# Causal attention between two quantised feed-forward blocks: two PSUM banks for scores, four for maxima, and one maximum operation for two heads

## The chip, the cores and the metric

The kernel runs on one core of a Trainium2 chip. The metric is the device time of one execution in microseconds (us); lower is better. TensorE is called PE here, VectorE DVE, ScalarE ACT, GpSimd POOL, and SP is the engine that issues the DMAs.

## The reference

The input is one sequence of 2048 tokens with 256 channels. A feed-forward block with 4-bit weights, causal attention with 16 heads of 16 channels, and the feed-forward block again are each added to it:

```python
x = x + 0.5 * ffn(layernorm(x))       # gate, up: 256 -> 2048, gelu(gate) * up, down: 2048 -> 256
x = x + attention(layernorm(x))       # 16 heads of 16 channels, causal softmax over 2048 keys
x = x + 0.5 * ffn(layernorm(x))       # weights: codes of 4 bits from a table, a scale for each 32
```

## The kernel before

The kernel is written engine by engine: each has a list of instructions in a fixed order, and semaphores with constant counts tie the lists together. Three stretches matter here.

**The first feed-forward block.** Twelve weight tiles are decoded (jobs 0 to 11). For each, ACT takes the bytes of the codes (`take_byte`) and the scales (`widen`), PE transposes both, ACT takes the codes back (`take_turned`), and DVE unpacks them (`decode`, five operations), scales them (`scale_weight`) and, after ACT has rounded them to a high part (`weight_high`), takes the low part (`weight_low`). The layer norm of the first 512 tokens (`variance`, `root`, `norm`, PE's `turn`, `split`) lies between jobs 0 and 1. The gate and up products (`gate_up`) start when the low parts of jobs 0 and 1 and that of the tokens are there. Each needs 128 of the 512 columns of a job.

**The attention.** It walks through 160 steps d. A step takes one group of four heads, one tile of 512 queries and one block of 128 keys. PE makes the scores of each head (`score(d, j)`, j = 0 to 3, keys by queries), ACT takes their exponential (L1175, `prob`), and PE multiplies the step before with the values (`weigh(d - 1)`, L815). The softmax needs the row maximum of each query ahead of its first step, so PE also makes the scores the other way round (`maxima(n)`, n = 0 to 639: one head, 128 queries, up to 512 keys), and DVE takes the maximum of each from PSUM: by a reduction off the diagonal (L1365), by an operation with the mask on it (L1368). Four or five `maxima` are placed in each step (`quota`), behind the scores j of the step by `CUTS`. For the steps with five the places are one, one, two, one; with four, one behind each score. The last one is step 136. PE's order in a step is so: score 0, maximum, score 1, maximum, score 2, one or two maxima, score 3, maximum, `weigh`.

PSUM has eight banks of 512 columns. In the attention, banks 3 to 5 hold scores (`S0`, `SBANKS`), banks 0 to 2 maxima (`M0`, `MBANKS`), bank 6 the output (`O0`), bank 7 the transposes (`X0`). Score n is written when exponential n - 3 is done, maximum n when the DVE has read maximum n - 3:

```python
elif SBANKS <= n < 4 * TAIL:
    pe.wait_ge(s["exp"], n - SBANKS + 1)
...
if n >= N_EARLY + N_BRIDGE + MBANKS:
    pe.wait_ge(s["max_read"], n - MBANKS + 1)
```

**The bridge.** In steps 3 to 7 banks 0 and 1 still hold the projection of the last 512 tokens (`LAST_UNITS`: four units at (4, 1), (5, 0), (6, 0) and (6, 2), where (d, j) is a step and the place behind its score j). The twelve maxima of these steps (`BRIDGE`) all go through bank 2. `last_block` is DVE's order there. When the fourth unit is done, SP writes the projections out and loads queries and keys, with many DMAs one behind the other, up to the row of maxima (`max_row(2)`) for which step 12 waits.

Of the kernel before, what the change touches and what calls it, by code (L numbers as in the profile page):

```python
# [45 lines left out]
SBANKS = 3  # L46
MBANKS = 3
# [5 lines left out]
def build_program(nc, h, Wq, bq, Wk, bk, Wv, bv, Wo, bo, gW, gS, uW, uS, dW, dS, out):  # L53
# [6 lines left out]
    with outer:  # L60
# [67 lines left out]
        def program(s, t):  # L128
# [53 lines left out]
            def chunk_order(n):  # L182
# [9 lines left out]
            BRIDGE = {(4, 0): 1, (4, 2): 1, (5, 0): 1, (5, 2): 1, (5, 3): 1, (6, 0): 1, (6, 1): 1, (6, 3): 1,  # L192
                      (7, 0): 1, (7, 1): 1, (7, 2): 1, (7, 3): 1}
# [90 lines left out]
            S0, M0, O0, X0 = 3, 0, 6, 7  # L284
# [21 lines left out]
            with ExitStack() as st:  # L306
# [85 lines left out]
                with nc.Block() as block:  # L392
# [217 lines left out]
                    def _(pe):  # L610
# [40 lines left out]
                        def gate_up(b, q, m):  # L651
                            k = b * NQ + q
                            if k >= 2:
                                pe.wait_ge(s["product"], k - 1)
                            elif m == 1:
                                pe.wait_ge(s["weight"], 2)
                            g, o = q // GT, (q % GT) * P
                            if b == 0 and q % GT == 0:
# [100 lines left out]
                        def maxima(n):  # L759
# [6 lines left out]
                            if n >= N_EARLY + N_BRIDGE + MBANKS:  # L766
                                pe.wait_ge(s["max_read"], n - MBANKS + 1)
                            elif n > N_EARLY:
                                pe.wait_ge(s["max_read"], min(n, N_EARLY + N_BRIDGE))
                                if n >= N_EARLY + N_BRIDGE:  # L770
                                    pe.wait_ge(s["full"], NU * NB)
                                    pe.wait_ge(s["v"], SUB * NB)
# [48 lines left out]
                        def gather(g):  # L821
                            pe.wait_ge(s["o_copied"], g + 1)
                            pe.wait_ge(s["x_free"], gather_use[g])
                            for i in range(SUB):
# [178 lines left out]
                    def _(act):  # L1003
# [31 lines left out]
                        def weight_high(n):  # L1035
                            act.wait_ge(s["weight"], n + 1)
                            nc.scalar.activation(w_hi[:, n, :, :], weight[:, n % 2, :, :], ACT.Copy).then_inc(s["w_hi"], 1)
# [80 lines left out]
                        for n in range(2):  # L1118
                            take_byte(n)
                            widen(n)  # L1120
                            take_turned(n)
                        root(0)
                        weight_high(0)
                        split(0)
                        weight_high(1)
                        take_byte(2)
                        widen(2)
                        for b in range(NB):
# [110 lines left out]
                    def _(dve):  # L1239
# [10 lines left out]
                        def scale_weight(n):  # L1250
                            dve.wait_ge(s["value"], n + 1)
                            dve.wait_ge(s["turned_s"], n + 1)
                            if n >= 2:
                                dve.wait_ge(s["w_lo"], n - 1)
                            nc.vector.scalar_tensor_tensor(weight[:, n % 2], mag[:, n % 2].bitcast(F16), 2.0 ** 14,
                                                           psum[:, decode_banks(n)[1], :].unsqueeze(1).broadcast_to([P, PL, BT]),
                                                           ALU.mult, ALU.mult).then_inc(s["weight"], 1)

                        def weight_low(n):
                            dve.wait_ge(s["w_hi"], n + 1)  # L1260
                            nc.vector.tensor_tensor(w_lo[:, n], weight[:, n % 2], as_f32(w_hi[:, n]), ALU.subtract).then_inc(s["w_lo"], 1)
# [91 lines left out]
                        def maxima(n):  # L1353
# [9 lines left out]
                            dve.wait_ge(s["max_scored"], n + 1)  # L1363
                            if c < qt:
                                nc.vector.tensor_reduce(to, psum[:, bank, :], AX.X, ALU.max).then_inc(s["max_read"], 1)  # L1365
                            else:
# [113 lines left out]
                        def last_block(d, mine):  # L1480
# [3 lines left out]
                            if d == 4:  # L1484
                                first_rest(u)
                                maxima(mine[1])
# [3 lines left out]
                            if d == 5:  # L1490
                                first_rest(u + 1)
                                maxima(mine[1])
# [10 lines left out]
                            if d == 7:  # L1503
                                third_part(u + 3)
                                maxima(mine[1])
# [147 lines left out]
```

## Time and profile before

| | |
|---|---|
| time, median of 3 runs | 1105.14 us (1104.61 to 1107.93) |
| the profiled execution's own time | 1102.31 us |
| its span, first to last instruction | 1100.6 us |
| mean granted clock of PE | 0.995 of full |
| PE busy | 1051.6 us (96%) |
| DVE busy | 692.0 us (63%) |
| ACT busy | 562.9 us (51%) |

The profile is one execution. A busy PE counts the modelled length of a matmul, which overlaps with the next one, so it is no measure of how far PE is from its best pace; the distances between starts are. L12 is line 12 of the kernel before.

### The profile page before, as it was taken

How to read it: one execution, taken by the hardware profiler on the slowest of the kernel's cores; microseconds unless marked ns; L12 is line 12 of the kernel's file. 1: busy time of each engine (PE TensorE's matmuls, PEld its weight loads, DVE VectorE, ACT ScalarE, POOL GpSimd, SP SyncE). 2: the span in 40 equal slices, each digit the busy share in tenths (PEclk: the TensorE clock that was granted, in tenths of full speed). 3: DMA queues.
4: the chain of work that ended last, by engine and by line, in shares of the span. 5: the costliest groups of instructions: out<-in, count | busy, mean ns of one | idle time of the engine just before them, and what ended most of it. 6: DMA issues, size and time to landing. Idle time of an engine off the chain costs nothing.

```text
span 1100.6 us, 16821 instructions
## 1 busy us (share of the span) xinstructions
PE 1051.6 (96%) x6240; PEld 673.0 (61%) x6240; DVE 692.0 (63%) x1589; ACT 562.9 (51%) x1028; POOL 95.6 (9%) x337
## 2 busy tenths in 40 slices
PE   4999999999998789999999999999999999999998
PEld 3888888887776423332223333333448888888887
DVE  5986544446566488899898988985424434343333
ACT  5664443442344646666667777777663334233222
POOL 0000000000002035221101102111110000000000
PEclk9999999999999989999999999999999999999999
DMA  7001040042140651212013012010000000000000
GB/s 198 2 1 34 1 134 1 10 139 55 27 129 14 168 122 35 69 50 54 1 34 73 16 39 54 2 39 2 1 1 1 1 20 1 1 20 1 20 1 20
DMA packets 85155, 43.75 MB, mean 40 GB/s; under 512 B 47954, under 2 KB 85074, under 8 KB 85074
## 3 DMA queue, kind: packets, MB, share of 16 engines
q1 hardware_dynamic: 85074, 42.69, 14.9%
q8 instruction: 49, 0.80, 0.3%
q14 instruction: 32, 0.26, 0.1%
HBM read 25.63 MB, written 16.78 MB: 39 GB/s over the span
## 4 chain that ended last, share of the span: by engine, by line
PE 79%; DVE 11%; ACT 2%; issue 2%; DMA 2%; SPq 2%; POOL 1%; ACTq 0%; POOLq 0%; DVEq 0%
PE psum L882 16%; PE psum L663 15%; PE psum L815 9%; PE psum L756 9%; PE psum L774 8%; PE psum L899 8%; PE psum L678 8%; DVE attn_part_max L1365 8%; PE psum L710 2%; PE psum L858 1%; PE psum L123 1%; DMA qk_rows<-qkv_parts 1%; ACT attn_prob L1180 1%; PE psum L722 1%; DMA attn_q<-attn_max_rows 1%
## 5 line engine op out<-in xcount | busy, mean ns | idle before, releaser
L1175 ACT ACTIVATE attn_prob<-psum 128x512 f32<-128x512 f32 (+3 forms) x548 | 257.0, 537 | 138.4 <-PE psum L756 135.7
L1365 DVE TENSOR_REDUCE attn_part_max<-psum 128x1 f32<-128x512 f32 x384 | 236.1, 683 | 13.7 <-PE psum L774 12.7
L663 PE MATMUL psum<-ffn_xt,all_w_hi 128*128 128x512 f32 x512 | 166.0, 406 | 0.0
L815 PE MATMUL psum<-attn_prob,attn_vals 128*32 128x512 f32 (+3 forms) x1280 | 151.2, 545 | 2.1 <-POOL attn_prob L585 0.8
L1368 DVE CUSTOM_DVE_ANT_0 attn_junk<-psum,attn_mask 128x128 bf16<-128x128 f32 (+3 forms) x256 | 114.6, 488 | 41.9 <-PE psum L774 41.1
L1471 DVE TENSOR_TENSOR ffn_act_out<-ffn_act_out,psum 128x512 f32<-128x512 f32 x64 | 44.1, 689 | 111.9 <-ACT ffn_act_out L1216 111.7
L1216 ACT ACTIVATE ffn_act_out<-psum 128x512 f32<-128x512 f32 x64 | 38.3, 598 | 130.1 <-PE psum L882 130.1
L663 PEld LDWEIGHTS psum<-ffn_xt,all_w_hi 128*128 128x128 f32 x512 | 91.5, 189 | 17.2
L678 PE MATMUL psum<-all_w_hi,ffn_inner 128*128 128x256 f32 x512 | 101.7, 283 | 0.1
L663 PE MATMUL psum<-ffn_xt,all_w_lo 128*128 128x512 f32 x256 | 101.6, 397 | 0.0
L899 PE MATMUL psum<-all_w_hi,ffn_inner 128*128 128x256 f32 x512 | 100.3, 280 | 0.1
L585 POOL TENSOR_SCALAR_AFFINE_SELECT attn_prob<-attn_prob 128x128 f32<-128x128 f32 x256 | 71.3, 292 | 312.6 <-ACT attn_prob L1175 264.6
L1060 ACT ACTIVATE ffn_act_out<-psum 128x512 f32<-128x512 f32 x64 | 38.2, 598 | 101.2 <-PE psum L663 101.0
L1304 DVE TENSOR_TENSOR ffn_inner<-ffn_act_out,ffn_inner 128x512 fp32r<-128x512 f32 x64 | 44.2, 691 | 71.2 <-ACT ffn_inner L1066 71.0
L678 PEld LDWEIGHTS psum<-all_w_hi,ffn_inner 128*128 128x128 f32 x512 | 82.6, 188 | 2.6 <-issue 0.4
L899 PEld LDWEIGHTS psum<-all_w_hi,ffn_inner 128*128 128x128 f32 x512 | 82.4, 188 | 2.9 <-DVE ffn_inner L1466 0.3
L882 PE MATMUL psum<-ffn_xt_even,all_w_hi 128*128 128x512 f32 x256 | 80.6, 396 | 0.0
L882 PE MATMUL psum<-ffn_xt_odd,all_w_hi 128*128 128x512 f32 x256 | 80.5, 395 | 0.0
L1466 DVE TENSOR_TENSOR ffn_inner<-ffn_act_out,ffn_inner 128x512 fp32r<-128x512 f32 x64 | 44.2, 691 | 52.0 <-ACT ffn_inner L1222 52.0
L678 PE MATMUL psum<-all_w_lo,ffn_inner 128*128 128x256 f32 x256 | 71.5, 279 | 0.0
L899 PE MATMUL psum<-all_w_lo,ffn_inner 128*128 128x256 f32 x256 | 71.5, 279 | 0.0
L1222 ACT ACTIVATE ffn_inner<-ffn_act_out 128x512 fp32r<-128x512 f32 x64 | 40.4, 632 | 52.9 <-PE psum L899 52.2
(148 smaller groups left out, 1618.6 us busy)
## 6 DMA issues: line engine op xcount, KB each, us to landing
qk_rows<-qkv_parts SPq DMA_DIRECT2D x16, 384.0 KB, 2.5
qk_rows<-qkv_parts SPq DMA_DIRECT2D x16, 256.0 KB, 3.0
attn_q_early<-qk_rows SPq DMA_DIRECT2D x8, 384.0 KB, 3.5
attn_k_early<-qk_rows SPq DMA_DIRECT2D x8, 384.0 KB, 4.7
attn_vals<-v_rows SPq DMA_DIRECT2D x48, 64.0 KB, 3.8
attn_k<-qk_rows SPq DMA_DIRECT2D x8, 384.0 KB, 3.7
attn_q<-qk_rows SPq DMA_DIRECT2D x8, 384.0 KB, 3.6
attn_k_late<-qk_rows SPq DMA_DIRECT2D x8, 384.0 KB, 3.5
```

Of the source, the lines that this page charges most:

```text
L585: nc.gpsimd.affine_select(out=tile, in_=tile, compare_op=ALU.is_ge, fill=0.0, base=0, pattern=[[1, P]], channel_multiplier=-1).then_inc(s[ ...
L663: last = nc.tensor.matmul(psum[:, 2 * m + q % 2, :], w_part[a][:, 3 * g + m, pl, o:o + P], xt[:, b % 2, c, pl, :], start=(n == 0), stop=(n ...
L678: last = nc.tensor.matmul(psum[:, ACC + i // 2, (i % 2) * H:(i % 2 + 1) * H], inner[:, a, q % 2, i * P:(i + 1) * P], w_part[e][:, 3 * (c / ...
L756: nc.tensor.matmul(psum[:, score_bank(n), at:BT], keys(key_load(g, c))[part, j, o * P:(o + 1) * P], queries(g)[part, j, at:BT], start=True ...
L774: nc.tensor.matmul(psum[:, max_bank(n), 0:cols], queries(g)[0:KR, hd, i * P:(i + 1) * P], keys(r)[0:KR, hd, 0:cols], start=True, stop=True ...
L815: last = nc.tensor.matmul(psum[32 * hd:32 * hd + 32, O0, at:BT], vals[:, r % KSLOTS * SUB + kb % SUB, VALUES_AT[hd]:VALUES_AT[hd] + 32], p ...
L882: last = nc.tensor.matmul(psum[:, 2 * m + q % 2, :], w_part[a][:, 3 * g + m, pl, o:o + P], xt2[b % 2][:, c, pl, :], start=(n == 0), stop=( ...
L899: last = nc.tensor.matmul(psum[:, ACC + i // 2, (i % 2) * H:(i % 2 + 1) * H], inner2[:, a, q % 2, i * P:(i + 1) * P], w_part[e][:, 3 * (c ...
L1175: nc.scalar.activation(prob[:, n % PRING, at:BT], psum[:, score_bank(n), at:BT], ACT.Exp).then_inc(s["exp"], 1)
L1304: nc.vector.tensor_tensor(inner[:, 1, k % 2, :], act_out[:, k % 2, :], as_f32(inner[:, 0, k % 2, :]), ALU.subtract).then_inc(s["inner_lo"], 1)
L1365: nc.vector.tensor_reduce(to, psum[:, bank, :], AX.X, ALU.max).then_inc(s["max_read"], 1)
L1368: nc.vector.tensor_tensor_reduce(out=junk[:, hd % 2, 0:cols], in0=psum[:, bank, 0:cols], in1=mask[:, BT - cols:BT], scale=1.0, scalar=STAR ...
```

## The change

Scores get two banks (4 and 5) instead of three, maxima four (0 to 3) instead of three. Score n now waits for exponential n - 2. Off the diagonal the maxima of heads 0 and 1, or 2 and 3, of a group lie in neighbouring banks, and DVE reduces both by one operation of two times 512 columns, when both are there; PE waits for banks only at the first of two. At the bridge there are eight maxima (in steps 4 to 6) instead of twelve, which alternate between banks 2 and 7; the others move to step 7, where four banks are free. In the start the norm comes ahead of job 0 on DVE, the first 128 columns of jobs 0 and 1 are scaled and split on their own (`first_scale`, `first_high`, `first_low`) and their other 384 afterwards, and a square root of a constant stands at the head of ACT's list.

```diff
-SBANKS = 3
-MBANKS = 3
+SBANKS = 2
+MBANKS = 4
...
-            BRIDGE = {(4, 0): 1, (4, 2): 1, (5, 0): 1, (5, 2): 1, (5, 3): 1, (6, 0): 1, (6, 1): 1, (6, 3): 1,
-                      (7, 0): 1, (7, 1): 1, (7, 2): 1, (7, 3): 1}
+            BRIDGE = {(4, 0): 2, (5, 0): 1, (5, 1): 1, (5, 3): 1, (6, 0): 1, (6, 1): 1, (6, 3): 1}
...
-            S0, M0, O0, X0 = 3, 0, 6, 7
+            S0, M0, O0, X0 = 4, 0, 6, 7
...
-                return 2 if n < N_EARLY + N_BRIDGE else M0 + n % MBANKS
+                return (2, X0)[n % 2] if n < N_EARLY + N_BRIDGE else M0 + n % MBANKS
...
-                            if b == 0 and q % GT == 0:
+                            if k == 0:
+                                pe.wait_ge(s["first_w_lo"], m + 1)
+                            elif b == 0 and (q == 1 or q % GT == 0):
...
                             if n >= N_EARLY + N_BRIDGE + MBANKS:
-                                pe.wait_ge(s["max_read"], n - MBANKS + 1)
+                                if hd % 2 == 0:
+                                    pe.wait_ge(s["max_read"], n - MBANKS + 2)
...
+                            elif n >= N_EARLY + 2:
+                                pe.wait_ge(s["max_read"], n - 1)
...
-                            dve.wait_ge(s["max_scored"], n + 1)
-                            if c < qt:
+                            pair = c < qt and n >= N_EARLY + N_BRIDGE
+                            if not pair or hd % 2:
+                                dve.wait_ge(s["max_scored"], n + 1)
+                            if pair and hd % 2:
+                                nc.vector.tensor_reduce(part_max[:, g % 2, hd - 1:hd + 1, i, c:c + 1], psum[:, bank - 1:bank + 1, :],
+                                                        AX.X, ALU.max).then_inc(s["max_read"], 2)
+                            elif c < qt and not pair:
...
+                        nc.scalar.activation(deviation[:, TT - 1:TT], nc.const_aps.tensor(1.0, [P, 1], F32), ACT.Sqrt)
...
                         variance(0)
+                        norm(0)
                         decode(0)
-                        norm(0)
+                        first_scale(0)
+                        decode(1)
+                        first_scale(1)
+                        split(0)
+                        first_low(0)
+                        first_low(1)
                         scale_weight(0)
-                        decode(1)
+                        scale_weight(1)
                         weight_low(0)
-                        split(0)
-                        scale_weight(1)
                         weight_low(1)
```

On DVE, late in the attention, behind the row maximum of a group (L1375 before, L1416 now), these rows stood before (`attn_part_max` is the tile of the maxima, L1365 the reduction off the diagonal; a row with x38 is 38 such operations in a row):

```order
L1375 TENSOR_REDUCE attn_row_max<-attn_part_max 128x16
L1365 TENSOR_REDUCE attn_part_max<-psum 128x1 x26
L1388 RECIPROCAL attn_rden<-psum 128x16
L1392 TENSOR_TENSOR all_heads<-psum,attn_rden 128x4x2x16 x2
L1365 TENSOR_REDUCE attn_part_max<-psum 128x1 x38
```

And these stand there now:

```order
L1416 TENSOR_REDUCE attn_row_max<-attn_part_max 128x16
L1403 TENSOR_REDUCE attn_part_max<-psum 128x2 x13
L1429 RECIPROCAL attn_rden<-psum 128x16
L1433 TENSOR_TENSOR all_heads<-psum,attn_rden 128x4x2x16 x2
L1403 TENSOR_REDUCE attn_part_max<-psum 128x2 x19
```

Each two reductions became one with two results; nothing else moved in that stretch, and PE's list in it is as before.

On DVE at the bridge (steps 4 and 5; `qkv_rest` and `qkv_parts` belong to the projection, the rows of L1368 are maxima with their mask) these rows stood before:

```order
L1368 ISA attn_junk,attn_part_max<-psum,attn_mask 128x128
L1368 ISA attn_part_max 128x1
L1336 TENSOR_TENSOR qkv_rest<-qkv_full,qkv_parts 128x512
L1368 ISA attn_junk,attn_part_max<-psum,attn_mask 128x128
L1368 ISA attn_part_max 128x1
L1331 TENSOR_TENSOR qkv_rows_v<-psum,qkv_bias_v 128x256 x2
L1340 TENSOR_TENSOR qkv_parts<-qkv_rest,qkv_parts 128x512
```

And now:

```order
L1409 ISA attn_junk,attn_part_max<-psum,attn_mask 128x128
L1409 ISA attn_part_max 128x1
L1409 ISA attn_junk,attn_part_max<-psum,attn_mask 128x128
L1409 ISA attn_part_max 128x1
L1372 TENSOR_TENSOR qkv_rest<-qkv_full,qkv_parts 128x512
L1367 TENSOR_TENSOR qkv_rows_v<-psum,qkv_bias_v 128x256 x2
L1376 TENSOR_TENSOR qkv_parts<-qkv_rest,qkv_parts 128x512
```

The second maximum moved ahead of the work that waits for ACT's part of the projection.

On ACT at the start, up to the first high part of the weights, these rows stood before:

```order
L1008 ACT_TABLE_LOAD
L1008 ACTIVATE decode_byte<-decode_early_codes 128x512
L1021 ACTIVATE attn_q_early<-decode_scales 128x512
L1032 ACTIVATE decode_turned<-psum 128x512
L1008 ACTIVATE decode_byte<-decode_early_codes 128x512
L1021 ACTIVATE attn_q_early<-decode_scales 128x512
L1032 ACTIVATE decode_turned<-psum 128x512
L1043 ACT_TABLE_LOAD
L1043 ACTIVATE all_deviation<-all_var_eps 128x4
L1037 ACTIVATE all_w_hi<-decode_weight 128x1024
L1054 ACTIVATE ffn_xt<-psum 128x1024
```

And now:

```order
L1132 ACT_TABLE_LOAD
L1132 ACTIVATE all_deviation<-const-float32-1.0 128x1
L1016 ACTIVATE decode_byte<-decode_early_codes 128x512
L1029 ACTIVATE attn_q_early<-decode_scales 128x512
L1057 ACTIVATE all_deviation<-all_var_eps 128x4
L1040 ACTIVATE decode_turned<-psum 128x512
L1016 ACTIVATE decode_byte<-decode_early_codes 128x512
L1029 ACTIVATE attn_q_early<-decode_scales 128x512
L1040 ACTIVATE decode_turned<-psum 128x512
L1051 ACTIVATE all_w_hi<-decode_weight 128x2x128
L1068 ACTIVATE ffn_xt<-psum 128x1024
```

The square root of the norm moved ahead of five activations, and the second load of a table is gone.

## Rows read from the trace of the kernel before

**Rows 1.** The page's part 2: granted clock of PE in 40 equal slices
```profile
PEclk9999999999999989999999999999999999999999
```

**Rows 2.** Windows: start:end, length, busy us (x instructions) of each engine, PEclk, DMA share
```profile
448.00:588.00 140.00, 135.74 (x793) 41.65 (x792) 127.66 (x304) 89.83 (x189) 22.47 (x85) 1.00 0.16 38
588.00:760.00 172.00, 170.17 (x1053) 55.16 (x1049) 148.72 (x359) 124.28 (x266) 25.42 (x97) 1.00 0.14 33
```

**Rows 3.** The page's part 4, the chain that ended last, by line
```profile
PE psum L882 16%; PE psum L663 15%; PE psum L815 9%; PE psum L756 9%; PE psum L774 8%; PE psum L899 8%; PE psum L678 8%; DVE attn_part_max L1365 8%; PE psum L710 2%; PE psum L858 1%; PE psum L123 1%; DMA qk_rows<-qkv_parts 1%; ACT attn_prob L1180 1%; PE psum L722 1%; DMA attn_q<-attn_max_rows 1%
```

**Rows 4.** Timeline, step with five maxima: start, length, engine, line [idle before]
```profile
563.50 0.39 PE L756 MATMUL psum<-attn_q_early,attn_k 99*128 99x512 bf16 x1
...
563.73 0.38 PE L774 MATMUL psum<-attn_k_early,attn_q 96*128 96x512 bf16 x1
...
563.99 2.15 ACT L1175 ACTIVATE attn_prob<-psum 128x512 f32<-128x512 f32 x4 [0.78 <-PE psum L756]
...
564.15 3.08 DVE L1365 TENSOR_REDUCE attn_part_max<-psum 128x1 f32<-128x512 f32 x5 [0.36 <-PE psum L774]
...
565.49 0.10 PEld L774 LDWEIGHTS psum<-attn_k_early,attn_q 96*128 96x128 bf16 x1 [0.49 <-DVE attn_part_max L1365]
...
565.81 1.06 PE L815 MATMUL psum<-attn_prob,attn_vals 128*32 128x512 f32 x8
...
566.81 0.39 PE L756 MATMUL psum<-attn_q_early,attn_k 99*128 99x512 bf16 x1
```

**Rows 5.** Timeline, a step with four maxima off the diagonal
```profile
710.49 1.06 PE L815 MATMUL psum<-attn_prob,attn_vals 128*32 128x512 f32 x8
...
711.98 2.06 ACT L1175 ACTIVATE attn_prob<-psum 128x512 f32<-128x512 f32 x4 [0.78 <-PE psum L756]
...
712.62 0.10 PEld L756 LDWEIGHTS psum<-attn_q_early,attn_k_late 99*128 99x128 bf16 x1 [0.15 <-ACT attn_prob L1175]
...
713.34 0.64 PE L815 MATMUL psum<-attn_prob,attn_vals 128*32 128x512 f32 x4
```

**Rows 6.** Timeline, `weigh` before and behind a step with four diagonal maxima
```profile
657.20 1.06 PE L815 MATMUL psum<-attn_prob,attn_vals 128*32 128x512 f32 x8
...
659.83 0.64 PE L815 MATMUL psum<-attn_prob,attn_vals 128*32 128x512 f32 x4
```

**Rows 7.** Lines by form, 440 to 760 us: count, busy us, mean ns
```profile
L1365 DVE TENSOR_REDUCE attn_part_max<-psum 128x1 f32<-128x512 f32 x336 | 206.2, 683 | 10.9 <-PE psum L774 10.0
L1175 ACT ACTIVATE attn_prob<-psum 128x512 f32<-128x512 f32 x328 | 171.7, 605 | 66.1 <-PE psum L756 65.3
```

**Rows 8.** Lines by form, 0 to 20 us
```profile
L1299 DVE TENSOR_TENSOR ffn_xt<-psum,ffn_xt 128x1024 fp32r<-128x1024 f32 x1 | 1.2, 1221 | 0.0
```

**Rows 9.** Timeline of the start
```profile
7.29 0.17 DVE L1276 TENSOR_SCALAR all_var_eps<-all_mean_var 128x4 f32<-128x4 f32 x1
...
8.46 0.29 DVE L1243 TENSOR_SCALAR attn_q_early<-decode_turned 128x512 uint16<-128x512 uint16 x1 [1.00 <-ACT decode_turned L1032]
...
9.39 0.69 DVE L1248 TENSOR_TENSOR attn_q_early<-attn_q_early,attn_vals 128x1024 uint16<-128x1024 uint16 x1
...
10.26 1.28 ACT L1043 ACT_TABLE_LOAD   x1
...
12.00 1.38 DVE L1292 TENSOR_SCALAR ffn_xb<-all_x,all_mean_var,all_rstd 128x256 f32<-128x256 f32 x4
...
21.50 1.20 PE L663 MATMUL psum<-ffn_xt,all_w_hi 128*128 128x512 f32 x2
...
27.75 0.29 DVE L1243 TENSOR_SCALAR attn_q_early<-decode_turned 128x512 uint16<-128x512 uint16 x1
```

**Rows 10.** Timeline of the bridge: a maximum's wait, and the fourth unit
```profile
363.08 0.23 PE L774 MATMUL psum<-attn_k,attn_q 96*128 96x128 bf16 x1 [0.49 <-DVE attn_part_max L1368]
...
371.94 1.75 PE L710 MATMUL psum<-ffn_xt,qkv_wt 128*128 128x512 f32 x6
```

**Rows 11.** The chain that ended last, in order of time: start, length
```profile
393.12 5.85 DMA attn_q<-attn_max_rows
```

More of the change, by code:

```diff
@@ L766, in maxima @@
                             if n >= N_EARLY + N_BRIDGE + MBANKS:
-                                pe.wait_ge(s["max_read"], n - MBANKS + 1)
[L768 to L772, printed above, removed]
+                                if hd % 2 == 0:
+                                    pe.wait_ge(s["max_read"], n - MBANKS + 2)
+                            elif n >= N_EARLY + N_BRIDGE:
+                                pe.wait_ge(s["max_read"], N_EARLY + N_BRIDGE)
+                                pe.wait_ge(s["full"], NU * NB)
+                                pe.wait_ge(s["v"], SUB * NB)
+                            elif n >= N_EARLY + 2:
+                                pe.wait_ge(s["max_read"], n - 1)
+                            elif n == N_EARLY + 1:
+                                pe.wait_ge(s["x_free"], turn_use[EARLY - 1] + 1)
                             cols = BT if c < qt else P * (i + 1)
@@ L1036, in weight_high, with first_high @@
                             act.wait_ge(s["weight"], n + 1)
-                            nc.scalar.activation(w_hi[:, n, :, :], weight[:, n % 2, :, :], ACT.Copy).then_inc(s["w_hi"], 1)
+                            cols = slice(P if n < 2 else 0, GT * P)
+                            nc.scalar.activation(w_hi[:, n, :, cols], weight[:, n % 2, :, cols], ACT.Copy).then_inc(s["w_hi"], 1)
+                        def first_high(n):
+                            act.wait_ge(s["first_weight"], n + 1)
+                            nc.scalar.activation(w_hi[:, n, :, 0:P], weight[:, n, :, 0:P], ACT.Copy).then_inc(s["first_w_hi"], 1)
                         def root(use):
@@ L1116, in copy_max @@
                             act.sem_inc(s["max_rows"], 1)
[L1118 to L1121, printed above, removed]
+                        nc.scalar.activation(deviation[:, TT - 1:TT], nc.const_aps.tensor(1.0, [P, 1], F32), ACT.Sqrt)
+                        take_byte(0)
+                        widen(0)
                         root(0)
-                        weight_high(0)
+                        take_turned(0)
+                        take_byte(1)
+                        widen(1)
+                        take_turned(1)
+                        first_high(0)
                         split(0)
-                        weight_high(1)
+                        first_high(1)
                         take_byte(2)
                         widen(2)
+                        weight_high(0)
+                        weight_high(1)
                         for b in range(NB):
@@ L1484, in last_block @@
                             if d == 4:
+                                maxima(mine[1])
                                 first_rest(u)
-                                maxima(mine[1])
                                 take_rows(i)
@@ L1490, in last_block @@
                             if d == 5:
+                                maxima(mine[1])
                                 first_rest(u + 1)
-                                maxima(mine[1])
                                 take_rows(i + 2)
@@ L1571, in _ @@
                                 split(Q_USE[NB - 1])
+                            if d == 7:
+                                third_part(NU * NB - 1)
                             if (d, 0) in BRIDGE:
@@ L1615, in build_program @@
         NORM = "aggr var std rstd xb "
-        W_SEMS = "ident turned_s wide turned_c byte turned weight w_hi w_lo step value scales0 scales1 scales2 "
+        W_SEMS = "first_weight first_w_hi first_w_lo ident turned_s wide turned_c byte turned weight w_hi w_lo step value scales0 scales1 scales2 "
         CODE_SEMS = " ".join(f"codes{n}" for n in range(3 * NG))
```

32 lines of the change are left out of this document (21 added, 11 removed).

## The prediction, made before the changed kernel had run

> **What bounds the kernel now.** I read the chain that ended last, the windows, the timeline of single steps, and then the waits at the start and the bridge. The chain lies on PE nearly everywhere; the one other line with a large share is DVE's reduction L1365 with 8% [rows 3]. In the attention two stretches differ. In the steps with five maxima DVE is the bound: the five reads take 3.08 us of a step of 3.31 (563.50 to 566.81), and PE waits 0.49 us for a bank of the last maximum [rows 4]. In the steps with four, PE is the bound: 2.85 from one weigh to the next, and the fourth score's bank comes free (712.62) before PE gets to it [rows 5]. ACT has 2.06 us of exponentials in such a step and is nowhere the bound. Steps 28 to 136 fill 448 to 760 us, 312 us of the span, at full clock [rows 2].
>
> So the change relieves DVE in the five-maxima steps, and takes a bank from the scores in all of them. Which of the two counts is settled by following a step.
>
> **A step's recurrence.** Times from score 0. From the rows: matmuls of 512 columns follow each other by 0.22; an exponential begins 0.49 after its score (563.50, 563.99), DVE's read 0.42 after its matmul (563.73, 564.15) [rows 4]; exponentials follow by 0.485 ((2.06 - 0.605) / 3), and a bank is free 0.64 after its exponential began (711.98, 712.62) [rows 5, 7]; weigh begins 0.32 after the last maximum (565.49, 565.81) and PE is free 1.00 later [rows 4].
>
> With four maxima before: eight matmuls, weigh at 1.85, next step at 2.85, as measured. Now score 2 needs exponential 0: 0.49 + 0.64 = 1.13 instead of 0.88. Score 3 needs exponential 1: 0.975 + 0.64 = 1.62 instead of 1.32. The last maximum comes at 1.84, weigh at 2.16, the next step at 3.16. That is **0.31 more**, and DVE's relief gives nothing back, since its reads were hidden here. With diagonal maxima the matmuls are shorter and a step takes 2.63 [rows 6]; score 3 still waits until 1.62, so that it ends at 2.99 to 3.16: 0.42 more on average.
>
> Here the Trainium skill has a rule, in PSUM — Partial Sum Buffer, section "PSUM bank collisions raise a hardware error": two engines must not touch a bank's quadrant at once, whatever the columns. So the score may not follow the exponential through the bank. The trace agrees, as the kernel waits for the whole exponential (0.64); if it could follow column by column, the four-maxima steps would stay at 2.85.
>
> **The price of a pair.** The trace has no reduction of 1024 columns. The 512-column one takes 0.683 [rows 7], DVE's 1024-column operation from PSUM 1.22 [rows 8]: 1.05 ns for a further element. A pair so costs 0.683 + 512 x 1.05 ns = 1.22, against 1.37 for two. Bounds: 1.07 if the fixed part vanished, and 1.37 if two banks cost two operations; I take 1.22, the nearest row. There are 368 such reads, so DVE saves 184 x 0.15 = 28 us of work, but a pair holds two banks for the whole read and begins only with its second score. With five maxima and an even start: the second maximum goes at 0.65, the read begins at 1.07 and ends at 2.29, and the fifth, which needs these banks, goes at 2.35; weigh 2.67, next step **3.67 instead of 3.31**. With an odd start the pair that began in the last step is read from 0.64 to 1.86, the fourth maximum waits for it until 1.92, score 3 and the fifth follow, and the step again ends at 3.67. If the read cost nothing, the score banks alone would hold the step at 3.33. The relief of DVE buys nothing even where DVE was the bound.
>
> VectorE: DVE Perf Modes, section "The TRN2 errata", in the Trainium skill gives 120 cycles and one for each element for an operation from PSUM and advises larger tiles, which speaks for the change. By it a pair would take 1.19 (an estimate from that page) and the step 3.64; the row for 512 columns is 0.02 above its figure.
>
> **The sum over the attention.** I carried the recurrence through all steps by the kernel's own placement of maxima, short scores, mask reads and row maxima. For the kernel before it stays within 3.5 us of the trace over the 312 us, so I trust it to tell the two kernels apart. Of steps 28 to 136, 53 have full scores and four maxima: 31 off the diagonal, 9.8 us more, and 22 on it, 9.3 more. 29 have full scores and five maxima: 7.2 more, 0.25 each and not 0.36, since 13 of them mix in diagonal reads and the others stand in short runs that begin behind short reads. The 27 steps with narrower scores change by 0 together, as their exponentials are shorter. Sum: **+26.3**. Steps 12 to 27 add 0.7. From step 137 on four banks serve the scores as before: 0.
>
> **The start.** DVE ends the variance at 7.46 and then waited for ACT's square root, which stood behind two jobs and a table load of 1.28 at 10.26 [rows 9]. Now the root is free at 7.8. DVE then: norm (1.38) to 9.4, decode (8.46 to 10.08, so 1.62) to 11.1, 256 columns (1.22 less 768 x 1.05 ns = 0.41) to 11.5, the same for job 1 to 13.5, split of the tokens behind ACT's copy of 1.0 to 14.9, two first low parts to 15.8. There the first products can start, before at 21.50. Then four pieces of 768 at 0.95 to 19.6, decode of job 2 to 21.2, its scaling to 22.4, the first product to 23.1. ACT's side (two high parts, three activations, a table load and a gelu) ends at about 22.4, just ahead. Decode of job 3 so begins at 23.1 instead of 27.75 [rows 9]: **-4.7**. Up to job 11 DVE is full, later PE, so the shift is kept. Bounds: -2.7 if ACT's side is 2 us later, -5.7 if PE's earlier start counts in full.
>
> **The bridge.** Before, each maximum went through bank 2 behind the last read, and that read stood on DVE behind a wait for ACT: PE's unit behind the maximum at 363.08 was held by it [rows 10]. With two banks and DVE's new order the unit waits only for the projection's own copies. Carried through with the same latencies, the fourth unit (371.94 [rows 10]) begins **3.1 us earlier**. Step 12 waits for a landing (393.12 + 5.85 [rows 11]) at the end of SP's list, which starts from that unit, so 3.1 is kept; what step 7 saves is covered by this wait. Bounds: 0, if SP's earlier stores hold its list, and 5.
>
> **Sum against the profiled execution's own time:** 1102.3 + 26.3 + 0.7 - 4.7 - 3.1 = 1121.5. The median of the runs shown is 2.8 above that execution; with part of that, **1123 us**, 1.6% slower than the median.
>
> **The rivals.**
> (a) The score bank wait does not bite, and the kernel is faster. This needs exponential 0 to free its bank 0.39 after its start, not 0.64, so that score 2 goes at 0.88. Then the four-maxima steps stay at 2.85, the attention loses some 3 us at the five-maxima steps, and the time is 1102.3 + 3.9 - 7.8 = 1098, with the offset 1101. For it: PE does little waiting for ACT now. Against: the load at 712.62 is marked as waiting for ACT exactly 0.64 behind [rows 5]. It decides below 0.06 us lost in a step. Chance 0.06.
> (b) The pair costs as much as two reads, 1.37. The five-maxima step becomes 3.81, DVE is late in the mixed ones too, and the recurrence gives 9 us more: 1132. For it: two banks in one operation stand in no row. Against: [rows 8] is a read over two banks and costs 1.22. Chance 0.12.
> (c) PE waits more, and the clock falls. In the slice around 400 us it is 8 tenths [rows 1], where step 12 waits. At the half clock a step's matmuls double; a tenth of the 312 us there costs about 30: 1150. Against: five-maxima steps have PE waiting 0.5 us of 3.31 now at full clock [rows 2, 4], and the new waits are of this size. Chance 0.04.
> (d) Score banks cost as said, but start and bridge give both upper bounds, 5.7 and 5, and a pair costs 1.07: the recurrence gives 6 us less, so 1102.3 + 20.3 + 0.7 - 10.7 = 1113, with the offset 1115. Chance 0.10.
>
> **Numbers.** The forecast has 0.68. 1112 to 1133 holds it with (b) and (d), about 0.9 less what I may have missed; I leave it there. A run of this kernel can tell 0.3% from no change, some 3 us. Faster by more than that is half of (a) and a rest, 0.05; within it the rest of (a), 0.03; slower 0.92.
>
> **What would show it.** The changed profile should have weigh to weigh 3.16 in the four-maxima steps, with PE's loads for scores 2 and 3 waiting for ACT, 3.67 in full five-maxima steps, with the wait for DVE's reduction on the fifth maximum; pairs of 1.22; DVE's busy time about 27 us lower; the third job's decode at 23; the fourth unit about 8 us earlier; and the full clock from 448 us on. Weigh to weigh of 2.85 with four maxima would prove me wrong at the root.

## The result, and the profile after

The changed kernel takes **1134.18 us** (median of 4 runs, 1131.85 to 1137.42), the kernel before, measured beside it, 1104.88 us (1103.06 to 1107.93): a ratio of **1.0259**, 95% interval 1.0225 to 1.0293. The profiled execution's own time is 1133.03 us, 30.7 us more than that of before, and its span 1131.2 us. The direction was forecast; the time is 1 us above the range, and the loss of 2.6% is larger than the 1.6% of the forecast.

The page after: the granted clock in 40 slices, the chain by engine and by line, and the group of the pairs (count, busy us, mean ns of one, idle before it).

```profile
PEclk9999999999998889999999999999999999999999
...
PE 78%; DVE 7%; ACT 7%; issue 3%; DMA 2%; SPq 2%; POOL 1%; ACTq 0%; DVEq 0%; POOLq 0%
PE psum L890 16%; PE psum L665 14%; PE psum L821 10%; PE psum L758 9%; PE psum L907 8%; PE psum L680 8%; PE psum L780 6%; ACT attn_prob L1194 5%; DVE attn_part_max L1403 4%; PE psum L712 2%; PE psum L123 1%; PE psum L866 1%; PE psum L724 1%; ACT attn_prob L1199 1%; DMA qk_rows<-qkv_parts 1%
...
L1403 DVE TENSOR_REDUCE attn_part_max<-psum 128x2 f32<-128x1024 f32 x184 | 218.4, 1223 | 43.7 <-PE psum L780 42.7
```

ACT's exponential L1194 is new in the chain with 5%, where before it had no such share [rows 3]; DVE's share went from the 8% of L1365 to 4% of L1403. A pair takes 1223 ns, as forecast.

The windows after (the columns are those of [rows 2]):

```profile
448.00:588.00 140.00, 125.21 (x717) 36.33 (x715) 114.81 (x191) 85.39 (x174) 20.95 (x76) 1.00 0.14 34
588.00:760.00 172.00, 162.55 (x938) 42.70 (x937) 132.39 (x239) 117.95 (x237) 21.59 (x80) 1.00 0.15 35
```

All of it is at the upper clock. PE is busy 287.76 us of these 312, before it was 305.91 [rows 2]: PE waits for its banks now, and the clock has no part in it.

A step with four maxima, timeline of the changed kernel, to be held against [rows 5]:

```profile
654.35 1.07 PE L821 MATMUL psum<-attn_prob,attn_vals 128*32 128x512 f32 x8
...
655.35 0.39 PE L758 MATMUL psum<-attn_q,attn_k_early 99*128 99x512 bf16 x1
...
655.83 2.17 ACT L1194 ACTIVATE attn_prob<-psum 128x512 f32<-128x512 f32 x4 [1.00 <-PE psum L758]
...
656.48 0.10 PEld L758 LDWEIGHTS psum<-attn_q,attn_k_early 99*128 99x128 bf16 x1 [0.59 <-ACT attn_prob L1194]
...
656.97 0.10 PEld L758 LDWEIGHTS psum<-attn_q,attn_k_early 99*128 99x128 bf16 x1 [0.37 <-ACT attn_prob L1194]
...
657.51 0.64 PE L821 MATMUL psum<-attn_prob,attn_vals 128*32 128x512 f32 x4
```

`weigh` to `weigh` is 657.51 - 654.35 = 3.16, to the hundredth the forecast. The exponential begins at 655.83, its bank is free at 656.48, 0.65 later, and score 2 goes then; the load for score 3 waits 0.37 for the next exponential.

A step with five maxima, against [rows 4]:

```profile
577.90 1.07 PE L821 MATMUL psum<-attn_prob,attn_vals 128*32 128x512 f32 x8
...
579.12 0.38 PE L780 MATMUL psum<-attn_k_early,attn_q 96*128 96x512 bf16 x1
...
579.61 3.50 DVE L1403 TENSOR_REDUCE attn_part_max<-psum 128x2 f32<-128x1024 f32 x3 [0.96 <-PE psum L780]
580.03 0.10 PEld L758 LDWEIGHTS psum<-attn_q_early,attn_k 99*128 99x128 bf16 x1 [0.59 <-ACT attn_prob L1194]
...
580.89 0.10 PEld L780 LDWEIGHTS psum<-attn_k_early,attn_q 96*128 96x128 bf16 x1 [0.74 <-DVE attn_part_max L1403]
...
581.65 1.07 PE L821 MATMUL psum<-attn_prob,attn_vals 128*32 128x512 f32 x8
```

3.75, forecast 3.67. The load at 580.89 waits 0.74 for the pair whose read began at 579.61 and lasted 1.22, although DVE had been idle for 0.96 before it: the pair had to wait for its second maximum (579.12), and held the bank of its first all that time.

Where the time went, by the start of `weigh` of single steps against before: 2.05 us earlier at step 1, 3.89 at step 12, 2.19 at step 27, then 11.26 us later at step 72, 30.61 at step 135 and 30.59 at step 158. So the loss lies in steps 28 to 136, and the tail costs nothing.

### The profile page after: what moved, and what is told of

Same layout as the page of the kernel before. It is cut to its first block, busy times and chain, and to the rows that moved or that the text cites. A ratio compares the mean times of both kernels' runs of the same rounds, so it can differ in the third digit from the quotient of the medians.

```text
span 1131.2 us, 16820 instructions
## 1 busy us (share of the span) xinstructions
PE 1066.1 (94%) x6240; PEld 664.2 (59%) x6240; DVE 687.1 (61%) x1409; ACT 575.7 (51%) x1030; POOL 96.9 (9%) x337
## 4 chain that ended last, share of the span: by engine, by line
PE 78%; DVE 7%; ACT 7%; issue 3%; DMA 2%; SPq 2%; POOL 1%; ACTq 0%; DVEq 0%; POOLq 0%
PE psum L890 16%; PE psum L665 14%; PE psum L821 10%; PE psum L758 9%; PE psum L907 8%; PE psum L680 8%; PE psum L780 6%; ACT attn_prob L1194 5%; DVE attn_part_max L1403 4%; PE psum L712 2%; PE psum L123 1%; PE psum L866 1%; PE psum L724 1%; ACT attn_prob L1199 1%; DMA qk_rows<-qkv_parts 1%
## 5 line engine op out<-in xcount | busy, mean ns | idle before, releaser
L1194 ACT ACTIVATE attn_prob<-psum 128x512 f32<-128x512 f32 (+3 forms) x548 | 269.8, 530 | 158.8 <-PE psum L758 153.2
L1403 DVE TENSOR_REDUCE attn_part_max<-psum 128x2 f32<-128x1024 f32 x184 | 218.4, 1223 | 43.7 <-PE psum L780 42.7
```

The lines of the kernel that those rows point to most:

```text
L1194: nc.scalar.activation(prob[:, n % PRING, at:BT], psum[:, score_bank(n), at:BT], ACT.Exp).then_inc(s["exp"], 1)
L1403: nc.vector.tensor_reduce(part_max[:, g % 2, hd - 1:hd + 1, i, c:c + 1], psum[:, bank - 1:bank + 1, :], AX.X, ALU.max).then_inc(s["max_rea ...
```

## The experiments

**Two banks for scores alone, and pairs taken out of the change.** The first kernel is the one before with

```diff
-SBANKS = 3
+SBANKS = 2
-            S0, M0, O0, X0 = 3, 0, 6, 7
+            S0, M0, O0, X0 = 4, 0, 6, 7
```

> The kernel before with one edit: the scores have banks 4 and 5 (SBANKS 2, S0 4), the maxima keep three banks and single reductions, start and bridge are as before. Theory (the bank of the scores sets the step): with four maxima off the diagonal weigh to weigh is 3.16 instead of 2.85, with five about 3.33 instead of 3.31 plus what the waits add, and the recurrence gives 23 us more over the attention: about 1128. Rival (the bank wait does not bite, and the pairs alone make the changed kernel slow): 1105, with 2.85 in the steps with four maxima.

Measured: 1126.5 us, ratio 1.0218 (1.0189 to 1.0247); steps with five maxima take 3.33. A step with four maxima in it (line L756 is the score, as before):

```profile
650.56 1.07 PE L815 MATMUL psum<-attn_prob,attn_vals 128*32 128x512 f32 x8
...
652.70 0.10 PEld L756 LDWEIGHTS psum<-attn_q,attn_k_early 99*128 99x128 bf16 x1 [0.59 <-ACT attn_prob L1175]
...
653.19 0.10 PEld L756 LDWEIGHTS psum<-attn_q,attn_k_early 99*128 99x128 bf16 x1 [0.38 <-ACT attn_prob L1175]
...
653.73 1.06 PE L815 MATMUL psum<-attn_prob,attn_vals 128*32 128x512 f32 x8
```

3.17 with the same two waits. The rival is out: this one edit gives most of the loss.

The second is the changed kernel without pairs:

```diff
-                            pair = c < qt and n >= N_EARLY + N_BRIDGE
+                            pair = False
...
-                                if hd % 2 == 0:
-                                    pe.wait_ge(s["max_read"], n - MBANKS + 2)
+                                pe.wait_ge(s["max_read"], n - MBANKS + 1)
```

> The changed kernel with each maximum off the diagonal read by its own reduction (683 ns) and PE waiting for one bank at a time; two banks for scores, four for maxima, start and bridge as changed. Theory (a pair frees its two banks too late, so pairs cost time on top of the score banks): the steps with four maxima stay at 3.16, those with five come from 3.75 to about 3.4, and the recurrence gives 11 us less than the changed kernel: 1123. Rival (the pairs relieve DVE and are worth something): DVE's busy time rises by 28 us and the time is the same as the changed kernel's or above it, 1134 to 1140.

Measured: 1116.63 us, ratio 1.0126 (1.0099 to 1.0154), further down than expected, since the steps with five came to 3.33 and not 3.4, and narrow ones gained. A step with five maxima in it:

```profile
563.64 1.06 PE L820 MATMUL psum<-attn_prob,attn_vals 128*32 128x512 f32 x8
...
565.29 2.48 DVE L1405 TENSOR_REDUCE attn_part_max<-psum 128x1 f32<-128x512 f32 x4 [0.24 <-PE psum L779]
...
565.78 0.10 PEld L758 LDWEIGHTS psum<-attn_q_early,attn_k 99*128 99x128 bf16 x1 [0.59 <-ACT attn_prob L1193]
...
566.26 0.10 PEld L758 LDWEIGHTS psum<-attn_q_early,attn_k 99*128 99x128 bf16 x1 [0.16 <-ACT attn_prob L1193]
...
566.97 0.64 PE L820 MATMUL psum<-attn_prob,attn_vals 128*32 128x512 f32 x4
```

3.33 instead of 3.75, and no load waits for DVE. Two reads of one bank each are better here than one read of two. DVE's busy time is 694.1 us, 7.0 above the changed kernel's 687.1, where the rival had 28.

**A cheaper pair.** The changed kernel, whose pair reads half of the columns (half of the keys are left out of those maxima):

```diff
-psum[:, bank - 1:bank + 1, :],
+psum[:, bank - 1:bank + 1, 0:256],
```

> The changed kernel with the read of a pair over 256 instead of 512 columns of each of its two banks, which leaves out half of the keys from those maxima; everything else as changed. The read then has 512 elements, as a single one had (683 ns). Theory (five-maxima steps wait for the end of a pair's read, four-maxima steps for the scores' banks): the steps with four stay at 3.16, those with five fall from 3.75 to about 3.35, and the time is 1134 less 13 to 16 us: 1118 to 1121. Rival (what holds the steps with five is that PE waits for a bank of the scores there too, whatever the read costs): 1130 to 1134.

Measured: 1114.55 us, ratio 1.0104 (1.0084 to 1.0123), some 3 us lower than expected. The read takes 693 ns, steps with five maxima 3.33, with four 3.16. That is what single reads give, so it is the length of the pair's read that the five-maxima steps wait for.

**The start and the bridge.** Three kernels: before with the new start, before with the new bridge, and before with both. Their edits are the start's hunks of the change, its hunks of `BRIDGE`, `max_bank`, `last_block` and of PE's waits for banks there, and both together, with `SBANKS`, `MBANKS` = 3 and single reductions.

> The kernel before with the new start alone (norm ahead of job 0, the first columns of jobs 0 and 1 apart, the root at the head of ACT's list). Theory (the start moves everything from the third job on by the 5.4 us that the changed kernel shows, and only stretches at half clock take from it): job 3's decode at 22.3, and the time 5.4 us below before, 1097.5, less by 1 to 3 us if the clock falls at the waits between 260 and 400 us: 1098 to 1101. Rival (step 12 waits for its transfer anyway, so that the start is hidden): 1103, the same as before.

> The kernel before with the new bridge alone (eight maxima through banks 2 and 7 in steps 4 to 6, the rest in step 7, DVE's new order); banks and single reductions as before. Theory (the new start and the new bridge together gave 6.2 us, of which the start has some 4): steps 3 to 6 get shorter by 3 to 4 us, step 12 keeps 1.5 to 3 of it: 1100 to 1102. Rival (the transfer for step 12 starts no earlier, or the clock falls in its wait instead): 1103, the same as before.

> The changed kernel with three banks for scores, three for maxima and single reductions as before: only the new start and the new bridge are left of the change. Theory (start and bridge gain what the changed trace shows ahead of step 12, and the banks cost the rest): steps 28 to 136 take what they take before, step 12 comes 3 to 4 us earlier than before, and the time is 1100 to 1102. Should PE stay at full clock between 262 and 393 us, where the changed kernel lost it for some 24 us, up to 1096. Rival (the start's 5.5 us and the bridge's 4 are always lost again at the waits ahead of step 12): 1104 to 1106, the same as before.

Measured: start **1097.81 us, ratio 0.9947** (0.9930 to 0.9964); bridge 1102.26, ratio 0.9995 (0.9978 to 1.0013), no difference that can be told; both **1096.85, ratio 0.9950** (0.9934 to 0.9967). In the start's profile `weigh` of step 1 comes 5.54 us earlier than before and that of step 135 5.44: the rival that step 12 hides it is out. The bridge's profile has the fourth unit here, against 371.94 before [rows 10]:

```profile
369.19 1.75 PE L709 MATMUL psum<-ffn_xt,qkv_wt 128*128 128x512 f32 x6
```

and its windows around and behind step 12 are these:

```profile
390.00:410.00 20.00, 16.21 (x103) 6.60 (x103) 14.39 (x60) 8.24 (x22) 6.38 (x24) 0.83 0.48 108
410.00:415.00 5.00, 5.00 (x23) 1.72 (x21) 3.54 (x11) 3.53 (x7) 0.00 (x0) 0.66 0.01 4
```

The fourth unit is 2.75 us earlier; `weigh` is 2.91 earlier at step 12, but 1.76 at step 20. The last row is a window behind step 12, with a granted clock of 0.66, where the kernel before had 1.00 in it. Step by step the loss lies in that window: `weigh` of step 14 (at 408.3) still comes 3.06 earlier than before, that of step 15 (at 413.2) only 1.76, and so it stays to the end. The profile with both edits has the same lists in these steps and a clock of 1.00 in them (its windows from 400 to 410 us), and there 7.82 at step 14 are 7.77 at step 15. So the lower clock took the 1.3 us; whether the bridge brings it about was not tried.

**The same kernel again.** No edit.

> The changed kernel itself, once more, for a second profile. Theory (the stretches at half clock at 262 and 348 us, and the 3 us that the first profile lost there, are one execution's, since the kernels with the new start that have the same instructions up to there did not have them all): weigh of step 1 comes some 4 to 5.5 us earlier than before instead of 2.05, and from there to the end the distances are those of the first profile: four-maxima steps 3.16, five 3.75. Rival (they belong to the changed kernel): 2 us earlier again.

Measured: 1130.78 us. `weigh` of step 1 comes 2.39 us earlier than before, of step 12 6.19, of step 27 4.49, and at step 135 it is 28.37 later: from step 27 on the two profiles of the changed kernel differ by 0.06 us, up to there by 2.30. Windows of the first profile of the changed kernel:

```profile
255.00:275.00 20.00, 17.84 (x91) 13.54 (x89) 17.19 (x52) 6.47 (x9) 0.83 (x4) 0.91 0.00 1
340.00:360.00 20.00, 17.44 (x106) 9.55 (x105) 9.03 (x34) 12.15 (x26) 4.83 (x16) 0.83 0.01 2
```

of the second:

```profile
255.00:275.00 20.00, 17.73 (x91) 13.60 (x90) 16.77 (x50) 6.46 (x9) 0.83 (x4) 0.91 0.00 1
340.00:360.00 20.00, 17.11 (x115) 10.16 (x113) 10.47 (x37) 13.77 (x29) 4.89 (x16) 1.00 0.01 2
```

and of the kernel with the start alone:

```profile
255.00:275.00 20.00, 16.89 (x92) 12.30 (x90) 18.62 (x54) 7.02 (x10) 0.83 (x4) 1.00 0.00 1
340.00:360.00 20.00, 16.07 (x108) 8.99 (x107) 10.77 (x38) 12.39 (x30) 4.79 (x16) 1.00 0.08 14
```

Between 340 and 360 us the lower clock was one execution's. At 262 it was there both times. Of the other eight profiles with the new start, five have 1.00 between 255 and 275 us (start, start with bridge, without pairs, half pairs, `weigh` cut in two) and three have 0.91 (the two with maxima placed anew, `weigh` moved), and one of the old start has 0.91 too (two banks for scores alone), so it does not belong to an order of work either. My theory was right for the one stretch, and its 4 us or more at step 1 did not come.

What the stretches cost can be read against the kernel without pairs, which has the changed kernel's list up to step 7 and a clock of 1.00 in both windows. Its `weigh` of step 1 is 4.32 us earlier than before, for 2.05 and 2.39. Its fourth unit, and below it that of the changed kernel's first profile:

```profile
363.58 1.75 PE L712 MATMUL psum<-ffn_xt,qkv_wt 128*128 128x512 f32 x6
```

```profile
367.12 1.75 PE L712 MATMUL psum<-ffn_xt,qkv_wt 128*128 128x512 f32 x6
```

The second profile has it at 365.50. PE's matmuls of the first profile stand 0.06 us behind those of the kernel without pairs up to 262 us, 1.41 at 266, and 3.54 from 350 on; in the second they stand 0.35, 1.92 and 1.92 behind. So the stretch at 262 cost 1.4 to 1.6 us, and with the one at 348 the first profile lost 3.5.

**Where in the step PE waits.** If a score waits since it comes too soon behind the one whose bank it takes, other work between them should help. Three kernels tried that. The first cuts `weigh`:

```diff
+                                if j == 1 and early_half(d):
+                                    weigh(d - 1, 0)
...
-                                weigh(d - 1)
+                                weigh(d - 1, 1)
...
-                            for hd in range(NHQ):
+                            for hd in (2 * half, 2 * half + 1):
```

> The changed kernel with weigh of the step before cut in two in steps 8 to 136: heads 0 and 1 behind score 1 and its maximum, heads 2 and 3 at the end of the step, so that 0.5 us of PE work lies between score 1 and score 2. Same banks, pairs, start and bridge. Theory (PE waits only since nothing lies between a score and the one that needs its bank): score 2 then comes 1.38 behind score 0, later than its bank (1.13), the steps with four maxima fall from 3.16 to 2.85, those with five from 3.75 to about 3.2, and the recurrence gives 31 us less: 1103. Rival (the two banks cost time through something else, such as contention of ACT and PE in PSUM, or the instruction count of weigh): little of the 30 us comes back, 1125 to 1134.

Measured: **1190.47 us**, ratio 1.0797 (1.0768 to 1.0826): worse by 56 us than the changed kernel, where 31 less were expected. Neither theory said so. The timeline shows why:

```profile
652.13 1.05 PE L821 MATMUL psum<-attn_prob,attn_vals 128*32 128x512 f32 x4
...
653.12 0.39 PE L758 MATMUL psum<-attn_q,attn_k_early 99*128 99x512 bf16 x1
```

The half with two heads (x4) takes 1.05 us, the whole with four (x8) 1.07 in the changed kernel. The four heads write to four groups of 32 partitions, and their matmuls run side by side, so that a half costs as much as the whole and each step has 1 us more of PE. With that work between them, scores and maxima do follow each other by 0.22 again in this stretch, and no load waits for its bank as in the changed kernel; but a four-maxima step takes 3.92 (650.17 to 654.09), for 3.16. The Trainium skill, TensorEngine Tiling (Array Packing), section "Tiling Modes", says that an array in 128x32 tiles is four tiles, which work in parallel; by that a half saves nothing, and the trace agrees. I had taken half the time for half the heads.

The second moves `weigh` whole, on the kernel without pairs:

```diff
+                                if j == 1 and 8 <= d < TAIL:
+                                    weigh(d - 1)
...
+            PLACES = {4: (1, 0, 1, 2), 5: (1, 0, 2, 2)}
```

> The kernel of the run singles with the whole weigh of the step before, uncut, behind score 1 in steps 8 to 136, and the maxima placed one, none, one, two (with five: one, none, two, two). Theory (cutting weigh in two was what cost time in the run split_after, as two heads take the 1.05 us that four take side by side; moving it whole costs nothing): weigh stays at 1.06 us for eight matmuls, the score that needs a bank comes 1.10 or more behind the one that holds it, steps with four take about 2.94 and the time is 1116.6 less 11: 1106. Rival (it is the place in the middle of the step, where weigh needs the last exponential sooner, that cost the time): 1140 or more.

Measured: 1108.48 us, ratio 1.0045 (1.0023 to 1.0066), 8 us below the kernel without pairs; from step 27 to 135 it loses 5.9 us against before. `weigh` is 1.07 again, and a step with four maxima takes 2.89:

```profile
724.57 1.07 PE L824 MATMUL psum<-attn_prob,attn_vals 128*32 128x512 f32 x8
...
726.65 0.10 PEld L762 LDWEIGHTS psum<-attn_q_early,attn_k_early 99*128 99x128 bf16 x1 [0.31 <-ACT attn_prob L1199]
...
727.46 1.06 PE L824 MATMUL psum<-attn_prob,attn_vals 128*32 128x512 f32 x8
```

The third and fourth leave `weigh` at the end and move a maximum from behind score 3 to behind score 1, without pairs and with them:

```diff
+            PLACES = {4: (1, 2, 1, 0), 5: (1, 1, 2, 1)}
```

`PLACES` says how many maxima stand behind scores 0 to 3; with pairs the five-maxima steps have (1, 2, 0, 2).

> The kernel of the run singles (two banks for scores, four for maxima, single reductions) with the four maxima of a four-maxima step placed one, two, one, none behind scores 0 to 3, instead of one behind each; steps with five as before. Theory (PE waits because the score that needs a bank comes sooner than the exponential frees it): score 2 then comes 1.10 behind score 0 and needs its bank at 1.13, score 3 1.54 behind score 0 and needs it at 1.62, the steps with four fall from 3.16 to about 2.95 and the recurrence gives 10 us less than singles: 1106. Rival (the waits are in the number of banks whatever the order): 1117.

> The changed kernel with the maxima placed one, two, one, none behind scores 0 to 3 in steps with four and one, two, none, two in steps with five; pairs and banks as changed. Theory (two separate waits, one for the scores' banks in steps with four and one for a pair's read in steps with five, both set by places): steps with four fall from 3.16 to some 3.0, those with five from 3.75 to about 3.6, and the recurrence gives 11 us less than the changed kernel: 1123. Rival (with pairs the order does not matter, as the read holds two banks anyway): 1134.

Measured: 1107.44 us without pairs, ratio 1.0038 (1.0023 to 1.0053), and 1120.23 with them, ratio 1.0151 (1.0127 to 1.0175). Without pairs a step with four maxima takes 2.95:

```profile
641.78 1.06 PE L824 MATMUL psum<-attn_prob,attn_vals 128*32 128x512 f32 x8
...
643.92 0.10 PEld L762 LDWEIGHTS psum<-attn_q,attn_k_early 99*128 99x128 bf16 x1 [0.37 <-ACT attn_prob L1197]
...
644.73 0.16 PEld L824 LDWEIGHTS psum<-attn_prob,attn_vals 128*32 128x32 f32 x8 [0.23 <-issue]
```

The first wait is 0.37 where it was 0.59. With pairs the steps with four take 2.94 to 2.95, those with five 3.53 and 3.75 by turns. The banks' price is a matter of place as well as of number, but no order that I tried gave all of it back over all steps.

**All steps together.** For steps 28 to 136 the distances between starts of `weigh` were summed for each kind of step, as differences in us to the kernel before (full: scores of 512 columns; narrow: the others; off and on: without and with maxima on the diagonal):

| steps | forecast | changed | two banks alone | without pairs | half pairs | placed, without pairs | placed, pairs | `weigh` moved |
|---|---|---|---|---|---|---|---|---|
| 22 full, four, on | +9.3 | +9.2 | +9.3 | +9.3 | +9.2 | +6.5 | +6.6 | +5.3 |
| 31 full, four, off | +9.8 | +10.8 | +10.2 | +10.5 | +10.5 | +4.0 | +5.6 | +0.1 |
| 29 full, five | +7.2 | +9.6 | +2.4 | +2.4 | +1.5 | +2.5 | +7.5 | -0.9 |
| 27 narrow | 0 | +3.6 | +1.6 | -1.5 | -1.8 | -4.1 | +2.6 | +1.6 |
| sum | +26.3 | +33.2 | +23.4 | +20.7 | +19.4 | +8.7 | +22.3 | +6.2 |

Two score banks with four maxima banks read one by one cost 20.7 us, and the pairs 12.5 more, all but 0.3 of these in steps with five maxima and in narrow ones. With `weigh` moved, the two banks cost nothing in the full steps with four maxima off the diagonal and 5.3 us in those on it.

## Why the prediction was right or wrong

**Which of the two counts: right.** The waits in the four-maxima steps (3.16), the unchanged tail and the full clock from 448 us on came out. Even the sentence that the score banks alone hold a five-maxima step at 3.33 did, in the kernel without pairs. Rival (a) has fallen with 3.16, and rival (c) with a clock of 1.00 from 448 us on. Behind the sentence on the rule for two engines in one bank the prediction says that the trace agrees. The trace can't say that: the score waits for the whole exponential because the kernel's semaphore says so, and no run lets it in earlier.

**The price of a pair: right for one, wrong for the saving.** 1223 ns against 1.22. Rival (b) would have had 1.37; its time of 1132 is near the result, but not for its reason. Wrong was the sentence that DVE saves 184 x 0.15 us = 28. DVE's busy time went from 692.0 only to 687.1 us, and in the kernel without pairs it is 694.1, so the pairs save 7.0. That sentence took the length of one read, where the distance of two reads in a row was the measure: 3.08 us for five less the last one's 0.683 is 0.60 apiece [rows 4, 7], and now 3.50 for three pairs (579.61), less 1.22, is 1.14 apiece. A pair saves 2 x 0.60 - 1.14 = 0.06 us, not 0.15. The row for this stood in the prediction's own groups. By the Trainium skill, VectorE: DVE Perf Modes, section "The TRN2 errata", a merged operation saves 120 cycles, 0.125 us (an estimate from that page); the trace does not agree, and the measured distance decides.

**The term that failed: "Sum: +26.3", measured +33.2.** The steps 28 to 136 were mis-sized by 6.9 us; the mechanism was right for the four-maxima steps and incomplete for the pairs. (1) The five-maxima step is 3.75 and not 3.67. A pair's read begins 0.49 after its second maximum's matmul (579.12, 579.61), where I had taken the 0.42 of a single one [rows 4]; the full five-maxima steps cost 9.6 for 7.2. (2) "The 27 steps with narrower scores change by 0 together, as their exponentials are shorter" is wrong: they cost 3.6. The exponential is shorter, the pair is not, since maxima are as wide there as elsewhere. With single reductions these steps even gain 1.5 us, and with half-length pairs 1.8, so that the length of the read costs 5 us here. (3) Full four-maxima steps cost 1 us more.

**Steps 12 to 27:** 1.7 for 0.7 in both profiles of the changed kernel. Two banks for scores alone lose 1.6 there (1.13 us earlier than before at step 12, 0.44 later at step 27), with a granted clock of 1.00 between 405.5 and 451.5 us. So the score banks explain it without the pairs and without the clock.

**The start: right as a mechanism, but "the shift is kept" failed in the changed kernel.** Job 3's decode is at 22.30 (23.1 forecast), 5.45 us earlier; alone the start gives 5.8 us by ratio, for a term of 4.7, and there the shift is kept. In the changed kernel's profiles 2.05 and 2.39 of it were left at step 1. With start and bridge and the old banks it is 5.39, with the new banks and single reads 4.32, both at the upper clock on the way from 255 us on: so 1.1 us are the banks in the first steps (made good by step 6, where these two have 8.24 and 8.59), and the other 2.3 and 1.9 the stretches of lower clock. The prediction had the clock only as a rival for steps 28 to 136, and no term for it ahead of them. The measured loss of 29.3 us is 3.9 below the 33.2 of steps 28 to 136, where start and bridge were to give 7.8 together.

**The bridge: right at the fourth unit** (2.75 earlier alone, 3.1 forecast; with the start 363.93, 8.0 earlier, for "about 8"; in the changed kernel itself 4.8 and 6.4 earlier, as the lower clock took its part), but the 3.1 were not kept: in its own profile 1.7 are left at the end, and the ratio shows none. The prediction had looked for a loss at SP's list, and the profile has it behind step 12, in a stretch of lower clock.

In sum, from 1121.5 to the profile's 1133.0: 6.9 us are the steps 28 to 136, 1.0 the steps 12 to 27, 2.7 the start up to step 1, and 1.2 the bridge up to step 12 (0.3 over the difference, as step 27 is in two of these sums).

The best version found is the kernel before with the new start, alone or with the new bridge: 0.5% faster. The banks and the pairs together cost more than five times what that gives (33.2 us against 6).

## What to carry to other kernels

Count banks by reach: a buffer is held from the first write to the end of the last read, latencies included (here 0.49 + 0.65 us for a score), and what counts is how much other work the producer has between two uses of it. One operation over two buffers holds both for the whole read and starts with the second, so it has to save more of the reader's fixed price for each operation than the longer hold costs; take that from the distance of operations in a row (0.60 us here), not from the length of one (0.683). Before work is cut into halves, see whether its parts ran side by side.

## What the runs showed of the hardware

Matmuls into four groups of 32 partitions ran side by side: 1.07 us for eight, 1.05 for four of them. The granted clock fell to its lower level about the same wait of PE in one kernel's execution and not in another's: the matmul behind a wait of 2.13 us for DVE stood at 262.18 in the changed kernel (window at 0.91) and at 262.05 with the start alone (window at 1.00):

```profile
262.18 0.98 PE L780 MATMUL psum<-attn_k_early,attn_q_early 96*128 96x384 bf16 x2 [2.13 <-DVE attn_part_max L1409]
```

```profile
262.05 0.81 PE L777 MATMUL psum<-attn_k_early,attn_q_early 96*128 96x384 bf16 x2 [2.13 <-DVE attn_part_max L1399]
```

The stretch behind it cost 1.4 us there. Two profiles of one kernel differed by 2.3 us at step 12, 1.6 of it from a stretch at 348 us that only one of them had, so a term of 1 or 2 us ahead of step 12 can't be read from one profile. Over whole executions the same shows: those of the kernel before that were taken beside the first experiments ran from 1099.46 us at a mean granted clock of 0.998 to 1107.84 at 0.988.
